# Expert-choice FFN of an audio tower: one expert of two batches per unit, row-paired mark products, gating split between ScalarE and VectorE

## The reference

```python
def _L0_ffn_ref(x, Wg, W1, b1, W2, b2):
    B, L, H, E, F, C = (8, 2048, 128, 8, 256, 2)
    b, l, h = x.shape                      # here 16, 748, 128
    k = min(max(int(l * C / e), 1), l)     # 187
    S = jax.nn.softmax(x @ Wg, axis=-1)
    St = jnp.swapaxes(S, 1, 2)
    G, I = jax.lax.top_k(St, k)
    ex = jnp.take_along_axis(x[:, None], I[..., None], axis=2)
    hmid = jax.nn.gelu(jnp.einsum('bekh,ehf->bekf', ex, W1) + b1[None, :, None, :], approximate=False)
    out = jnp.einsum('bekf,efh->bekh', hmid, W2) + b2[None, :, None, :]
    vals = G[..., None] * out
    new_x = jnp.zeros_like(x).at[jnp.arange(b)[:, None, None], I].add(vals)
    return new_x
```

## Time and profile before

| What | Value |
|---|---|
| Time, median of 3 runs (lowest to highest) | 2656.92 us (2653.99 to 2658.15) |
| Span of the profiled execution, first to last instruction | 2655.1 us |
| What lies around that span | not listed for this execution; the median stands 1.8 us above the span |
| PE, DVE, ACT, POOL busy over the span | 90%, 76%, 63%, 42% |
| Stage of `chosen_ffn` | 1261.8 to 1640.3 us |

### The profile page before, as it was taken

One profiled execution on the slowest core, in us unless ns is written; L12 is line 12 of the kernel. 1 busy time (PEld: TensorE's weight loads), 2 busy tenths in 40 slices (PEclk: granted clock), 3 DMA queues, 4 the chain that ended last, 5 costly groups with the idle time before them and its releaser, 6 DMA issues. The chain is left out here.

```text
span 2655.1 us, 52098 instructions
## 1 busy us (share of the span) xinstructions
PE 2389.5 (90%) x16443; PEld 1819.7 (69%) x16443; DVE 2026.5 (76%) x3647; ACT 1665.8 (63%) x3127; POOL 1124.6 (42%) x1338
## 2 busy tenths in 40 slices
PE   7989699999999999854899997999849999999993
PEld 7989455444445444343799997888738887888882
DVE  4555589999999999489688887788776666787775
ACT  3345267777777777743566664555527777777772
POOL 0016002223223222323777773444337774666664
PEclk9999699999999999975899998999969999999997
DMA  3108633333333323054111112400021113777749
GB/s 90 36 12 319 193 56 50 62 62 56 48 62 62 57 47 62 18 152 149 42 38 38 39 38 68 164 0 0 1 81 52 51 52 103 243 240 247 243 143 277
DMA packets 161298, 249.19 MB, mean 94 GB/s; under 512 B 41645, under 2 KB 106902, under 8 KB 154233
## 3 DMA queue, kind: packets, MB, share of 16 engines
q1 hardware_dynamic: 128888, 208.77, 29.1%
q0 software_dynamic: 19712, 38.13, 4.9%
q10 hardware_dynamic: 12544, 0.39, 0.2%
HBM read 155.24 MB, written 93.41 MB: 94 GB/s over the span
## 5 line engine op out<-in xcount | busy, mean ns | idle before, releaser
L1014 ACT ACTIVATE probs<-score 128x748 f32<-128x748 f32 (+1 forms) x768 | 568.4, 794 | 117.2 <-PE score L839 115.8
L943 DVE TENSOR_REDUCE part_max<-to_dve 128x1 f32<-128x512 f32 (+1 forms) x768 | 479.7, 683 | 84.0 <-PE to_dve L820 83.6
L2762 DVE TENSOR_TENSOR m_hid_lo<-m_up,m_hid_hi 128x512 fp32r<-128x512 f32 x408 | 279.9, 687 | 157.1 <-ACT m_hid_hi L2735 157.1
L820 PE MATMUL to_dve<-k_stack,q_stack 48*128 48x512 f32 (+3 forms) x1536 | 351.4, 367 | 20.9 <-DMA k_stack<-k_parts 20.1
L839 PE MATMUL score<-q_stack,k_stack 49*128 49x374 f32 (+1 forms) x1536 | 317.3, 389 | 3.1 <-ACT probs L1014 1.0
L839 PEld LDWEIGHTS score<-q_stack,k_stack 49*128 49x128 f32 (+1 forms) x1536 | 162.0, 181 | 225.0 <-ACT probs L1014 199.7
L876 PE MATMUL o_sum<-probs,v_sb 128*17 128x374 f32 (+1 forms) x3072 | 315.6, 483 | 0.1
L2658 POOL DMA_INDIRECT e_sums<-m_gated,m_row_in x216 | 212.6, 984 | 162.3 <-DVE m_gated L2780 109.2
L820 PEld LDWEIGHTS to_dve<-k_stack,q_stack 48*128 48x128 f32 (+1 forms) x1536 | 223.1, 187 | 79.7 <-DVE part_max L943 36.6
L740 POOL TENSOR_TENSOR o_rows<-o_raw,inverse 128x384 f32<-128x384 f32 x32 | 26.9, 842 | 589.7 <-DVE inverse L953 589.7
L1371 POOL DMA_INDIRECT f_row_in_c<-c_rows,c_ids x192 | 218.4, 1137 | 75.2 <-issue 49.6
(11 more groups left out here) (411 smaller groups left out, 6003.8 us busy)
## 6 DMA issues: line engine op xcount, KB each, us to landing
m_weights<-e_records SPq DMA_DIRECT2D x54, 1028.0 KB, 6.9
q_stack<-q_parts SPq DMA_DIRECT2D x192, 93.5 KB, 3.1
k_stack<-k_parts SPq DMA_DIRECT2D x192, 93.5 KB, 4.2
e_slots<-blank SPq DMA_DIRECT2D x54, 260.0 KB, 3.9
m_row_in<-e_slots SPq DMA_DIRECT2D x54, 260.0 KB, 3.3
m_weights<-e_sums SPq DMA_DIRECT2D x16, 640.0 KB
e_records<-l_parts SPq DMA_DIRECT2D x16, 512.0 KB, 3.7
v_rows<-v_out SPq DMA_DIRECT2D x16, 408.0 KB, 5.9
```

Source lines behind the costliest of these rows:

```text
L820: last = pe.matmul(ring[i % RING][0:ROWS[c], at_col:at_col + keys.stop - keys.start], q_stack[its_slot][rows, j, c * P:c * P + ROWS[c]], k ...
L943: dve.tensor_reduce(part_max[0:ROWS[c], k, j, c, 0:1], ring[i % RING][0:ROWS[c], :], AX.X, ALU.max).then_inc(used, 1)
L1014: act.activation(probs[0:n, s % 2, m, 2 * j:2 * j + 2, :], score[tile][0:n, :, 0:HALF], ACT.Exp).then_inc(tile_used, 1)
L2762: dve.tensor_tensor(hid_lo[:, f % RING, :], up[f % UPS][:, :], hid_hi[:, f % RING, :].bitcast(F32), ALU.subtract).then_inc(lo_done, 1)
```

## The change

A unit becomes one expert of two batches: 64 slots of the even batch on partitions 0 to 63 and 64 slots of the odd batch on 64 to 127. There are 64 units as before, and 8 groups of 8 units in place of 16 groups of 4.

- `widen` and `narrow` use one expert's weights for all 384 columns, 12 matmuls a unit in place of 24. `up` is one PSUM bank in place of two, and `widen` is issued in two halves, with `turn_rows` and `narrow` between them.
- `combine` turns round: the gated rows are the weights (64 rows, 128 columns) and the marks stream. The lower 64 partitions sum into `sums[0]` (even batch), the upper 64 into `sums[1]` (odd batch), and the two are issued next to each other. The output now has features on partitions, tokens in columns.
- So the sums must be turned: after 8 units ACT copies `sums[0]` and DVE `sums[1]` to SBUF (`take`), and in the three iterations that follow PE transposes four tiles each (`spread`) into `turn`, the bank that `turn_rows` and `split_x` use too; DVE adds four tiles at a time to `h` (`give_back`) and takes statistics in three later iterations (`measure`).
- The gate of a slot is now one column of the gathered row, since both halves have the same expert. `pick_gate` and `weigh` go; ACT multiplies by the gate as it rounds (3 instructions), DVE multiplies and subtracts in one (3 instructions). Both read PSUM.
- The ring of gathered rows is 8 units, freed when the unit is gated rather than when it is transposed.
- In `choose` the tables are laid out for the new order, and one table of indices is made by two instructions of 64 partitions.

```diff
-    UNIT_TILES = SLOT_TILES * 2 // E_N
-    PER_BATCH = E_N // 2
-    UNITS_C = B * PER_BATCH
-    COLS = 2 * SLOTS_E
     H = P // 2
-    RING = 5
-    BANKS = TILES // 2
-    BANDS = [slice(H * j, min(T, H * (j + 1) + T - k_tokens)) for j in range(UNIT_TILES)]
+    UNIT_TILES = SLOTS_E // H
+    PAIRS_B = B // 2
+    UNITS_C = PAIRS_B * E_N
+    COLS = UNIT_TILES * P
+    RING = 8
+    GROUP = 4
+    GROUPS_C = 2 * TILES // GROUP
+    BANDS = [slice(H * j, min(T, -(-(H * (j + 1) + T - k_tokens) // 2) * 2)) for j in range(UNIT_TILES)]
...
+        def gate(n, j):
+            return row_in[:, n % RING, j, P + expert_of(n):P + expert_of(n) + 1]
...
+        def returning(k):
+
+            m, at = divmod(k - 2, E_N)
+            return (m - 1, at) if 1 <= m <= PAIRS_B and at < 2 * GROUPS_C else None
...
-                def gather(n):
+                for n in range(UNITS_C):
                     if n >= RING:
-                        pool.wait_ge(turned, n - RING + 1)
+                        pool.wait_ge(gated_n, n - RING + 1)
...
+                    for i, (a, x) in enumerate([(w1_hi, x_hi), (w1_hi, x_lo), (w1_lo, x_hi)]):
+                        last = pe.matmul(up[:, 0:COLS], a[:, e * C_BLOCKS + k, :], x[:, n % 2, :], start=(i == 0), stop=(i == 2))
+                    last.then_inc(up_done, 1)
...
-                    for c in tiles:
-                        for j in [j for j in range(UNIT_TILES) if c in REACH[j]]:
-                            last = pe.matmul(sums[0:ROWS[c], c // 2, c % 2, :, :], marks[:, n % 2, j, c * P:c * P + ROWS[c]],
-                                             gated[:, n % 2, j, :, :], start=(i == 0 and j == 0 and c % 2 == 0),
-                                             stop=(i == PER_BATCH - 1 and j == UNIT_TILES - 1 and c % 2 == 1))
+                    for j in range(UNIT_TILES):
+                        for half, cols in pieces(n, j):
+                            for part in range(2):
+                                for o, rows_at in enumerate([slice(0, H), slice(H, P)]):
+                                    last = pe.matmul(sums[o][:, half, cols.start - half * HALF:cols.stop - half * HALF],
+                                                     gated[rows_at, n % 2, j, part, :], marks[rows_at, n % 2, j, cols],
+                                                     start=(e == 0 and j == 0 and part == 0),
+                                                     stop=(e == E_N - 1 and j == UNIT_TILES - 1 and part == 1))
+                    last.then_inc(combined, 1)
+
+                def spread(m, group, bank):
+                    if group == 0:
+                        pe.wait_ge(act_took, m + 1)
+                        pe.wait_ge(dve_took, m + 1)
+                        pe.wait_ge(padded, 1)
+                    for i in range(GROUP):
+                        o, c = divmod(group * GROUP + i, TILES)
+                        last = pe.transpose(bank[:, i * P:(i + 1) * P], summed[:, o, c * P:(c + 1) * P], g.ident[:, :])
+                    last.then_inc(spread_out, 1)
 
                 for k in range(-1, UNITS_C + 2):
                     if valid(k):
-                        widen(k)
+                        widen(k, 0)
+                    if valid(k + 1):
+                        if returning(k) and 1 <= returning(k)[1] <= GROUPS_C:
+                            pe.wait_ge(added, returning(k)[0] * GROUPS_C + returning(k)[1])
+                        turn_rows(k + 1)
                     if valid(k - 1):
                         narrow(k - 1)
-                    if valid(k + 1):
-                        turn_rows(k + 1)
+                    if valid(k):
+                        widen(k, 1)
+                    if returning(k) and returning(k)[1] < GROUPS_C:
+                        m, group = returning(k)
+                        if valid(k + 1):
+                            pe.wait_ge(split, k + 2)
+                        spread(m, group, turn)
...
-                    act.copy(gated[:, n % 2, :, 0, :], weighed[:, n % 2, :, :]).then_inc(gate_hi, 1)
+                    for j in range(UNIT_TILES):
+                        last = act.activation(gated[:, n % 2, j, 0, :], back[:, j, :], ACT.Copy, scale=gate(n, j))
+                    last.then_inc(gate_hi, 1)
...
                     dve.wait_ge(gate_hi, n + 1)
-                    dve.tensor_tensor(gated[:, n % 2, :, 1, :], weighed[:, n % 2, :, :],
-                                      gated[:, n % 2, :, 0, :].bitcast(F32), ALU.subtract).then_inc(gated_n, 1)
+                    for j in range(UNIT_TILES):
+                        last = dve.scalar_tensor_tensor(out=gated[:, n % 2, j, 1, :], in0=back[:, j, :], scalar=gate(n, j),
+                                                        in1=gated[:, n % 2, j, 0, :].bitcast(F32), op0=ALU.mult, op1=ALU.subtract)
+                    last.then_inc(gated_n, 1)
```

More of the change, by code:

```diff
@@ new lines, in narrow @@
+                def narrow(n):
+                    e = expert_of(n)
+                    if n:
+                        pe.wait_ge(kept, n)
+                    for k in range(C_BLOCKS):
+                        pe.wait_ge(lo_done, C_BLOCKS * n + k + 1)
+                        for i, (a, x) in enumerate([(w2_hi, hid_hi), (w2_hi, hid_lo), (w2_lo, hid_hi)]):
+                            last = pe.matmul(down[:, 0:COLS], a[:, e * C_BLOCKS + k, :], x[:, n % 2, k, :],
+                                             start=(k == 0 and i == 0), stop=(k == C_BLOCKS - 1 and i == 2))
@@ L1457, in _ @@
+                    if returning(k) and returning(k)[1] < GROUPS_C:
[3 more added lines that the diff above has]
+                        spread(m, group, turn)
                     if valid(k - 2):
-                        combine(k - 2, range(TILES))
+                        combine(k - 2)
                     if valid(k - 1):
                         turn_back(k - 1)
+                for group, bank in enumerate([turn, up, down]):
+                    spread(PAIRS_B - 1, group, bank)
@@ L1592, in _ @@
                     if valid(k):
-                        split_hid(k, 1)
-                    if done is not None:
-                        measure(done // PER_BATCH)
-                give_back(B - 1)
-                measure(B - 1)
+                        split_hid(k, 0)
+                    if returning(k) and returning(k)[1] < GROUPS_C:
+                        give_back(*returning(k), turn)
+                    elif returning(k):
+                        measure(returning(k)[0], returning(k)[1] - GROUPS_C)
+                    if valid(k - 1):
+                        mark(k - 1, 2)
+                    if valid(k):
+                        split_hid(k, 1)
+                take(PAIRS_B - 1)
+                for group, bank in enumerate([turn, up, down]):
+                    give_back(PAIRS_B - 1, group, bank)
+                for group in range(GROUPS_C):
+                    measure(PAIRS_B - 1, group)
 def load_small(nc, loads, tag):
```

223 lines of the change are left out of this document (85 added, 138 removed).

## The result

| Kernel | Median (lowest to highest) | Ratio to before, 95% interval |
|---|---|---|
| before | 2655.45 us (2653.16 to 2658.15) | |
| changed | 2635.07 us (2633.33 to 2637.03) | 0.9919 [0.9905, 0.9933] |

The median of before rests on one execution more than the one in the table ahead of the prediction (2656.92 from three). The change takes 20.4 us off. The forecast was 2640.5. The profiled execution took 2637.03 us with a span of 2635.3, 19.8 less than the span of before.

The account below looks back on a forecast made before the run. PE was taken as the bound. The loop goes from 351.4 to 334.1 us (63 x 4.89 + 25.2 + 0.8); with 2 less at the start and 2.7 more at the end, 16.6 less: 2640.5 us, range 2624 to 2664.

Parts of the forecast that it names:

- The likeliest case: The change works as worked out, within the bounds of switch and ACT: 2632 to 2650 us, chance 0.50.
- Wide matmuls: `widen` and `narrow`: 12 matmuls of 384 columns at 0.176 us replace 24 of 192, 0.58 us less a unit.
- Pairs: `combine`: a pair of 64-row products costs one matmul, weight loads hidden; twelve pairs take 1.75 us a unit.
- Rival 5: Pairs' weight loads not hidden, 2725 us, or the two run one after the other, 2750 us; chance 0.06.
- Switches: PE's change between whole-array and half-array matmuls, twice a unit: 0.19 us each, bounds 0.10 and 0.30.
- Rival 4: The array empties fully at each mode change; a loss above 0.32 us a switch, 2673 us at 0.45; chance 0.12.
- ACT and DVE: Scaled gate instructions 0.25 us apart on ACT, 0.27 on DVE; the engines sum to 3.4 and 3.6 us a unit.
- rival 3: No change because DVE and ACT come late: ends at 2652 to 2662 us; chance 0.15.
- Unit: PE's time for one unit in the loop: 4.89 us against 5.21 before.
- Returns: Seven returns of sums in the loop, 3.6 us each: PE waits for `split_x` 0.5, 0.5 and 1.25 us, plus transposes.
- Start: Stage start: DVE's first instruction 0.6 us earlier, wide matmuls at half clock save about 1.3; 2 us less taken.
- End: Stage end: one `take`, four transposes, three additions and twelve statistics, 6.1 us against 3.4, so 2.7 us more.

Follow-up runs that it names:

- halves: Changed kernel with `widen` and `narrow` in 192 columns again, 24 matmuls a unit in place of 12 of 384: 2656.52 us, ratio 1.0007 to before.
- serial: Changed kernel with all 12 products of the lower 64 partitions issued first, then all 12 of the upper: 2722.16 us, ratio 1.0257 to before.
- switch4: Changed kernel with tile 0's products ahead of the transposes back, the others behind, so four mode changes a unit instead of two: 2650.21 us.
- x_first: Changed kernel with DVE doing `split_x` ahead of the two sets of marks in iterations that return sums: 2624.14 us, ratio 0.9887 to before.
- spread_late: Changed kernel with transposes of the sums behind the products and the addition to `h` at the end of DVE's iteration: 2621.82 us.
- tail_fill: Changed kernel with sixteen idle transposes of the identity ahead of the last unit's products: 2634.1 us in one execution.
- before_again: The kernel before, unchanged, run again for a second trace: 2658.62 us in one execution.
- gate_dve: Changed kernel with the gate back on DVE as one multiply, ACT rounding and DVE subtracting 384 columns: 2636.18 us, ratio 0.9935 to before.

## Why the prediction was right

The likeliest case came out (2632 to 2650 us, chance 0.50), in the stage that it named and by its mechanism. Point by point, predicted against the trace:

- **Wide matmuls**, 0.176 apart: 0.174. Right, and halves undoes it at 0.54 a unit. The forecast takes the saving 63 times and the waits of the returns apart from it; halves shows that for this term alone 42 times is right, because the returning iterations absorb it.
- **Pairs**, 0.17, 0.14 and 0.12 apart: 0.171, 0.146 and 0.114. serial shows that this is what carries the change. Rival 5 falls. The Trainium skill (TensorE: Matmul & The Clock Gate, Part 3: Packing small matmuls) says that a weight load overlaps running matmuls only when its row group differs. This case disagrees: in serial, with twelve products in a row on the same 64 rows, the loads stayed hidden, 0.172 us for 374 columns.
- **Switches**, 0.19 each: 0.20 in (0.269 instead of 0.174 from the last wide matmul to the first product, and 0.276 instead of 0.17 from there to the second pair) and 0.14 out (0.255 and 0.165 instead of 0.17 and 0.109). switch4 confirms the pair at 0.38 in place. Rival 4 asked for over 0.32 a switch and is refuted. The Trainium skill (TensorEngine Tiling (Array Packing), Key Properties) says that a change of tiling mode drains the TensorE; whatever happens at the change, it costs 0.20 and 0.14 us here.
- **ACT and DVE**, 0.25 and 0.27 apart: 0.26 and 0.26. They fit into the unit, and no quiet unit waits for either engine; rival 3 falls. The two `take`, 0.69 and 0.86 us apart in the sum, have records of 0.79 and 0.94, as assumed.
- **Unit**, 4.89: 4.85 us.
- **Returns**, 3.6 us with waits of 0.5, 0.5 and 1.25: 3.8 us (6.61 + 5.88 + 5.87 less 3 x 4.85), and ahead of the sums PE stands 1.2, 0.5 and 0.5 us longer than a slot. The place, the releaser and the size are right, and x_first and spread_late take them away.
- **Start**, 2 us less: 2.2, and the size is partly luck. The first gather did not come earlier: in both kernels it starts 1.30 us after DVE's cast to the table of indices (`c_ids`), so the 0.6 us that the prediction took from DVE there were not to be had. The wide matmuls at the half clock are worth 1.1 us (the start is 22.4 us in halves, 21.3 in the changed kernel; 1.3 was predicted). The other 1.1 us were not in the sum. They may come from the new order, in which the second unit's rows are transposed 14.0 us after `twice_c` in place of 15.2, but no run undoes the order alone.
- **End**, 2.7 us more: 4.1. The sum of work was right (tail_fill ends 2.6 later than before); the missing 1.5 us is the last unit's products at the half clock, which the prediction didn't consider. The earlier trace rows could not have shown it: before, the clock was at full there.

The stage's sum was 16.6 less; the traces say 17.4. That these are so near is in part luck: the loop gained 1.9 us more than the 17.3 forecast (most of it by a unit of 4.85 in place of 4.89), and the end lost 1.4 more. The forecast's own sum, 2638.5 and 1.8, is 2640.3, not 2640.5. It lies 5.2 us above the median of the changed kernel. Of these 0.8 us are the stage's and 1.5 the median of before, which was 2656.92 us from three executions and is 2655.45 from four. For the other 3 us no step of the sum answers (before_again).

What the forecast missed is what could be had: with the order of a few DVE or PE steps changed, 11 to 13 us more.

## What to carry to other kernels

A term worked out per unit must not be multiplied by all units: ask first in which iterations that engine waits, because there a cheaper or dearer slot ahead of the wait changes only the wait (halves), while one behind it counts in full (serial). A new periodic step (here the return of sums) belongs where its operand has long been ready and its bank is free for longest; moved behind the products and into another bank, it cost its own 0.44 us and nothing more in two of three iterations. Half-array products paid here because the two halves ran at the same time; a change of mode went into the sum at 0.14 to 0.20 us.

## What the runs showed of the hardware

- Matmuls on different halves of the array start out of program order: in serial the first product of the upper 64 rows started ahead of three of the lower 64 that stand before it, in all 64 units. In the changed kernel nothing hangs on it, since the records of the last products of the two halves end within 0.02 us of each other; whether ends can change places too was not tried.
- Weight loads of 128 columns were hidden behind a matmul on the same 64 rows (in serial 0.172 us from start to start for 374 columns, 0.114 to 0.122 for 246). The first pair after a change from whole to half array has a record 0.11 us longer (0.44 against 0.33), which I read as its load exposed.
- The granted clock fell to 1.2 GHz at the stage's end after PE had stood idle for 0.8 and 1.9 us around 2 us of work; with the second gap filled it stayed at 2.4 GHz. Gaps of 0.7 and 1.8 us in gate_dve left it there too, so nearly equal gaps went either way.
